# One kernel for a decoder layer: row statistics and the joint of mixer and feed-forward rearranged

## The reference

```python
x = x + mamba_block(layernorm(x), ...)                # "front" stage of the kernel
x = x + mlstm(layernorm(x), ctx, ctx, ...)            # "mixer"
x = x + ffn(layernorm(x), w_gate, w_up, w_down)       # "feed-forward"

# mlstm, per batch and head (4 heads of 64 channels, 256 tokens)
C = (q k^T / 8) * exp(log_D - max_log_D)
h = (C / max(|sum C|, exp(-max_log_D))) v
h_norm = (h - mean(h)) / sqrt(mean((h - mean(h))**2) + 1e-5)  # over the 64 channels
out = h_norm * (1 + out_w)

# ffn: every linear quantises both operands to a 4-bit grid in blocks of 16
layernorm(x) = (x - mean) / sqrt(var + 1e-5)          # per token, over 256 channels
gate, up = fp4_linear(x, w_gate), fp4_linear(x, w_up) # 704 hidden columns
y = fp4_linear(silu(gate) * up, w_down)
```

## Time and profile before

| | us |
|---|---|
| median of 3 runs | 604.32 (603.13 to 605.93) |
| profiled execution | 606.77, of which the span of instructions 605.1 |
| PE busy | 567.9 (94%) |
| DVE busy | 446.4 (74%) |
| ACT busy | 270.1 (45%) |
| POOL busy | 144.6 (24%) |

### The profile page before, as it was taken

How to read it: one execution, slowest core, us unless ns; L and a number is a source line. 1 busy time by engine, 2 the same in 40 slices (tenths; PEclk the granted TensorE clock), 3 DMA queues, 4 the chain that set the end, 5 groups by cost and what they waited for, 6 DMA issues and landing times. The chain is left out here.

```text
span 605.1 us, 9377 instructions
## 1 busy us (share of the span) xinstructions
PE 567.9 (94%) x2995; PEld 459.4 (76%) x2995; DVE 446.4 (74%) x990; ACT 270.1 (45%) x565; POOL 144.6 (24%) x209
## 2 busy tenths in 40 slices
PE   7989998999999899999999999989959899999995
PEld 6766666788888788888888888877855577777774
DVE  6986598379888324755655857575788999999994
ACT  2655877785788422222111112434434444444431
POOL 4120001134545021210110010005775222122200
PEclk8989999799999999999999999998977999999999
DMA  8300101000000093000000000011100000000000
GB/s 301 121 1 18 35 15 39 22 25 5 6 7 0 2 298 90 1 1 0 1 1 1 1 0 1 4 43 33 35 2 0 2 17 17 14 12 17 18 19 26
DMA packets 21392, 18.90 MB, mean 31 GB/s; under 512 B 12008, under 2 KB 20584, under 8 KB 20968
## 3 DMA queue, kind: packets, MB, share of 16 engines
q1 hardware_dynamic: 20920, 18.36, 9.5%
q10 hardware_dynamic: 432, 0.03, 0.1%
HBM read 16.04 MB, written 2.34 MB: 30 GB/s over the span
## 5 line engine op out<-in xcount | busy, mean ns | idle before, releaser
L923 PE MATMUL ps<-xnT,w_fc 128*128 128x256 f32 x512 | 112.8, 380 | 0.0
L923 PEld LDWEIGHTS ps<-xnT,w_fc 128*128 128x128 f32 x512 | 96.5, 190 | 12.7
L1658 PE MATMUL ps<-w_fc,scores 128*128 128x352 f32 x256 | 82.3, 476 | 1.5 <-ACT scores L1747 1.5
L1658 PEld LDWEIGHTS ps<-w_fc,scores 128*128 128x128 f32 x256 | 48.9, 196 | 29.0 <-ACT scores L1747 3.6
L1166 ACT ACTIVATE xs<-ps 128x512 f32<-128x512 f32 x32 | 19.1, 597 | 95.8 <-PE ps L923 75.7
L1279 DVE SCALAR_TENSOR_TENSOR fold<-xpad,conv_w,fold 128x256 f32<-128x256 f32 x120 | 50.9, 481 | 2.4 <-ACT fold L1068 1.6
L1677 PE MATMUL ps<-u_res,hT 128*128 128x256 f32 x192 | 44.2, 380 | 3.8 <-DVE scores L1856 2.8
L1677 PEld LDWEIGHTS ps<-u_res,hT 128*128 128x128 f32 x192 | 36.3, 190 | 11.3 <-issue 3.0
L806 PE MATMUL ps<-xnT,fold 128*128 128x256 f32 x160 | 39.2, 393 | 1.6 <-ACT xpad L1062 0.8
L806 PEld LDWEIGHTS ps<-xnT,fold 128*128 128x128 f32 x160 | 30.7, 198 | 9.5 <-issue 3.6
L813 PE MATMUL ps<-fold,xnT 128*128 128x512 f32 x64 | 36.8, 708 | 0.0
(11 more groups left out here) (299 smaller groups left out, 1208.8 us busy)
## 6 DMA issues: line engine op xcount, KB each, us to landing
zs<-in_ffn_w SPq DMA_DIRECT2D x1, 2112.0 KB, 10.9
x_res<-in_x SPq DMA_DIRECT2D x8, 256.0 KB, 7.6
w_fc<-in_w_fc SPq DMA_DIRECT2D x1, 2048.0 KB, 10.3
xnT<-in_ctxT SPq DMA_DIRECT2D x8, 256.0 KB, 3.1
xs<-in_ctx SPq DMA_DIRECT2D x16, 128.0 KB, 3.0
xs<-in_ctxT SPq DMA_DIRECT2D x8, 256.0 KB, 3.1
out<-scores SPq DMA_DIRECT2D x16, 128.0 KB, 1.7
fold<-in_w_in SPq DMA_DIRECT2D x2, 580.0 KB, 6.6
```

The lines of the kernel that those rows point to most:

```text
L923: last = pe.matmul(bank[half + r][:, i * S:(i + 1) * S], m.w_fc1[:, kk, col:col + P], m.xnT[:, b, kk * S:(kk + 1) * S], start=(kk == 0), s ...
L1658: last = pe.matmul(bank[1 + j][:, 0:HALF], xT[:, p, k * P:(k + 1) * P], m.w_gu[:, k, j * HALF:(j + 1) * HALF], start=(k == 0), stop=(k == ...
```

## The change

Three things are done.

- The row statistics of the feed-forward's layer norm move from its rounds into the mixer, a batch (two tiles) at a time: on DVE `row_stats` (lag 4, two statistics and two aggregates) between `weights` and `normalise`; on POOL `row_rstds` (lag 4, one addition, one power and two multiplications) ahead of `rstds`. The results are kept for all 16 tiles. The rounds have no statistics left, and POOL has nothing in them.
- `squares` becomes eight Squares of 64 columns, each with an accumulated sum. DVE's `variance` is gone.
- `pipelines` is gone. The joint is written out engine by engine. On DVE the first two tiles' `step_x` parts are spread over mixer steps 6 to 8; rounds 3 and 4 are cut and stand around mixer steps 9 and 10; round 5 stands ahead of the last `row_stats` (step 11); rounds 6 to 15 are the loop. On PE `gate_up(0)` stands ahead of the last batch's `sums`.

```diff
--- before.py
+++ after.py
...
-def pipelines(eng, units, stages, next_units, next_stages, begin, overlap):
...
@@ -1516,7 +1499,7 @@
-    BEGIN, OVERLAP = B - 1, 5
+    ROUNDS_APART = 6
...
-    st = sb("f_st", [P, 2, 6])
-    mv = sb("f_mv", [P, 2, 2])
-    ve = sb("f_ve", [P, 2, 1])
-    rstd = sb("f_rstd", [P, 2, 1])
-    shift = sb("f_shift", [P, 2, 1])
+    st = sb("f_st", [P, 2, C, 6])
+    mv = sb("f_mv", [P, T, 2])
+    ve = sb("f_ve", [P, T])
+    rstd = sb("f_rstd", [P, T])
+    shift = sb("f_shift", [P, T])
...
+    def rounds(eng, stages, first):
+
+        for r in range(first, ROUNDS_APART):
+            step(T, stages, r)
+        steady(eng, T, stages, ROUNDS_APART, T)
+        for r in range(T, T + depth_of(stages)):
+            step(T, stages, r)
...
@@ -1698,10 +1689,23 @@
-        forward = [(turn_x, 2), (lambda t, p: turn_down(0 if t == 0 else 2) if round_at(t) and t < 2 else None, 2),
-                   (turn_h, 4), (gate_up, 2), (lambda t, p: turn_down(1) if round_at(t) and t == 0 else None, 2),
-                   (down, 4)]
-        pipelines(pe, B, mixer, T, forward, BEGIN, OVERLAP)
+        forward = [(turn_x, 2), (turn_h, 4), (gate_up, 2), (down, 4)]
+        for k in range(B):
+            step(B, mixer, k)
+        last, p = B - 1, (B - 1) % 2
+        scores1_even(last, p)
+        scores0(last, p)
+        scores1_odd(last, p)
+        turn_x(0, 0)
+        sums(last - 1, 1 - p)
+        turn_down(0)
+        gate_up(0, 0)
+        sums(last, p)
+        turn_x(1, 1)
+        turn_down(1)
+        gate_up(1, 1)
+        turn_down(2)
+        rounds(pe, forward, 4)
...
         def squares(b, p):
             act.wait_ge(s["h_read"], LEAD + b + 1)
+            act.wait_ge(s["v_rstd"], LEAD + b - 1)
             act.wait_ge(s["v_ready"], LEAD + b)
-            act.activation(sq[:].rearrange("p g e -> p (g e)"), h[:, p, :, :].rearrange("p g e -> p (g e)"),
-                           ACT.Square).then_inc(s["sq_ready"], 1)
-
+            for i in range(C * XH):
+                last = act.activation(sq[:, i, :], h[:, p, i, :], ACT.Square, accum_out=var[:, p, i:i + 1])
+            last.then_inc(s["v_ready"], 1)
...
-            act.activation(xf[:, p, :], row(m.x_res, t), ACT.Identity, bias=shift[:, p, :], scale=rstd[:, p, :])\
+            act.activation(xf[:, p, :], row(m.x_res, t), ACT.Identity, bias=shift[:, bass.ds(t, 1)],
+                           scale=rstd[:, bass.ds(t, 1)])\
                .then_inc(f["xf_norm"], 1)
...
-        forward = [(turned_x, 2), (lambda t, p: save_down(0 if t == 0 else 2) if round_at(t) and t < 2 else None, 2),
-                   (turned_h, 4), (lift_x, 1), (lift_h, 3), (silu, 2),
-                   (lambda t, p: save_down(1) if round_at(t) and t == 0 else None, 2), (norm, 0)]
-        pipelines(act, B, mixer, T, forward, BEGIN, OVERLAP)
+        forward = [(turned_x, 2), (turned_h, 4), (lift_x, 1), (lift_h, 3), (silu, 2), (norm, 0)]
+        for k in range(B - 1):
+            step(B, mixer, k)
+            if k == B - 3:
+                norm(0, 0)
+            if k == B - 2:
+                norm(1, 1)
+                lift_x(0, 0)
+        last, p = B - 1, (B - 1) % 2
+        exps(last, p)
+        turned_x(0, 0)
+        squares(last - 2, p)
+        save_down(0)
+        squares(last - 1, 1 - p)
+        lift_x(1, 1)
+        norm(2, 0)
+        silu(0, 0)
+        turned_x(1, 1)
+        save_down(1)
+        squares(last, p)
+        lift_x(2, 0)
+        lift_h(0, 0)
+        silu(1, 1)
+        save_down(2)
+        norm(3, 1)
+        rounds(act, forward, 4)
...
-        def variance(b, p):
-            dve.wait_ge(s["sq_ready"], LEAD + b + 1)
-            dve.wait_ge(s["v_rstd"], LEAD + b - 1)
-            dve.tensor_reduce(var[:, p, :], sq[:], AX.X, ALU.add).then_inc(s["v_ready"], 1)
-
...
-        def tile_stats(t, p):
-            dve.wait_ge(s["x2_ready"], LEAD + t + C - p)
-            carry(dve, m)
-            dve.bn_stats(st[:, p, :], row(m.x_res, t)).then_inc(f["f_stats"], 1)
-
-        def tile_mean(t, p):
-            dve.wait_ge(f["f_stats"], LEAD + t + 1)
-            carry(dve, m)
-            dve.bn_aggr(mv[:, p, :], st[:, p, :]).then_inc(f["f_mv_ready"], 1)
+        def row_stats(b, p):
+            dve.wait_ge(s["x2_ready"], LEAD + C * (b + 1))
+            for c in range(C):
+                last = dve.bn_stats(st[:, p, c, :], m.x_res[:, C * b + c, :])
+            last.then_inc(f["f_stats"], 1)
+            dve.wait_ge(f["f_stats"], LEAD + b + 1)
+            for c in range(C):
+                last = dve.bn_aggr(mv[:, C * b + c, :], st[:, p, c, :])
+            last.then_inc(f["f_mv_ready"], 1)
...
-        first = [stage for k in range(5) for stage in ((step_x(k), 1), (step_h(k), 3))]
-        last = [stage for k in range(6, 9) for stage in ((step_x(k), 1), (step_h(k), 3))]
+        def parts(begin, end):
+            return [stage for k in range(begin, end) for stage in ((step_x(k), 1), (step_h(k), 3))]
+
+        def rows_steps(t, begin, end):
+            for k in range(begin, end):
+                step_x(k)(t, t % 2)
...
-        mixer = [only(3, lambda: chain.a_tokens(dve, TOKENS[0]).then_inc(m.gates_done, 1)),
+        begin = [only(3, lambda: chain.a_tokens(dve, TOKENS[0]).then_inc(m.gates_done, 1)),
                  only(4, lambda: chain.nm_tokens(dve, TOKENS[1]).then_inc(m.gates_done, 1)),
-                 (lambda b, p: weights(b, p, 0), 1), (lambda b, p: weights(b, p, 1), 1), (variance, 3),
-                 only(1, lambda: chain.sums(dve, *SECOND_HALF)), (normalise, 2),
-                 (scale, 3), only(2, lambda: chain.maxima(dve))]
-        forward = [(product, 3), *first, (tile_stats, 0), (output, 5), (tile_mean, 0), *last]
-        pipelines(dve, B, mixer, T, forward, BEGIN, OVERLAP)
+                 (lambda b, p: weights(b, p, 0), 1), (lambda b, p: weights(b, p, 1), 1), (row_stats, 4),
+                 only(1, lambda: chain.sums(dve, *SECOND_HALF))]
+        end = [(normalise, 2), (scale, 3), only(2, lambda: chain.maxima(dve))]
+        forward = [(product, 3), *parts(0, 5), (output, 5), *parts(6, 9)]
+        for k in range(B + 1):
+            step(B, begin, k)
+            if k == B - 2:
+                rows_steps(0, 0, 3)
+            elif k == B - 1:
+                rows_steps(0, 6, 9)
+            elif k == B:
+                rows_steps(1, 0, 3)
+            step(B, end, k)
+            if k == B - 2:
+                rows_steps(0, 3, 5)
+            elif k == B:
+                rows_steps(1, 3, 9)
+        step(T, [(product, 3), *parts(0, 1)], 3)
+        step(B, begin, B + 1)
+        step(B, end, B + 1)
+        step(T, [*parts(1, 9)], 3)
+        step(T, [(product, 3), *parts(0, 2)], 4)
+        step(B, begin, B + 2)
+        step(B, end, B + 2)
+        step(T, [*parts(2, 9)], 4)
+        step(T, forward, 5)
+        step(B, begin, B + 3)
+        rounds(dve, forward, 6)
...
-        def tile_rstd(t, p):
-            pool.wait_ge(f["f_mv_ready"], LEAD + t + 1)
-            carry(pool, m)
-            pool.tensor_scalar(ve[:, p, :], mv[:, p, 1:2], LN_EPS, None, ALU.add).then_inc(f["f_ve_ready"], 1)
-            pool.wait_ge(f["f_ve_ready"], LEAD + t + 1)
-            pool.tensor_tensor(rstd[:, p, :], ve[:, p, :], m.minus_half[:, 0:1], ALU.pow).then_inc(f["f_rstd_ready"], 1)
-            pool.wait_ge(f["f_rstd_ready"], LEAD + t + 1)
-            pool.wait_ge(f["xf_norm"], LEAD + t - 1)
-            carry(pool, m)
-            pool.tensor_scalar(shift[:, p, :], mv[:, p, 0:1], rstd[:, p, :], -1.0, ALU.mult, ALU.mult)\
-                .then_inc(f["f_shift_ready"], 1)
-
-        mixer = [(rstds, 3), (residual, 3)]
-        forward = [(tile_rstd, 0)]
-        pipelines(pool, B, mixer, T, forward, BEGIN, OVERLAP)
+        def row_rstds(b, p):
+            here = slice(C * b, C * (b + 1))
+            pool.wait_ge(f["f_mv_ready"], LEAD + b + 1)
+            pool.tensor_scalar(ve[:, here], mv[:, here, 1], LN_EPS, None, ALU.add).then_inc(f["f_ve_ready"], 1)
+            pool.wait_ge(f["f_ve_ready"], LEAD + b + 1)
+            pool.tensor_tensor(rstd[:, here], ve[:, here], m.minus_half[:, 0:C], ALU.pow).then_inc(f["f_rstd_ready"], 1)
+            pool.wait_ge(f["f_rstd_ready"], LEAD + b + 1)
+            for t in range(C * b, C * (b + 1)):
+                pool.tensor_scalar(shift[:, t:t + 1], mv[:, t, 0:1], rstd[:, t:t + 1], -1.0, ALU.mult, ALU.mult)\
+                    .then_inc(f["f_shift_ready"], 1)
+
+        mixer = [(row_rstds, 4), (rstds, 3), (residual, 3)]
+        for k in range(B + 4):
+            step(B, mixer, k)
```

## The result

The changed kernel takes 621.03 us (median of 4, 616.59 to 622.75), the kernel before 605.01: a ratio of 1.026, 95% interval 1.0213 to 1.0306, 16.0 us slower. Forecast was 618.8. Medians in this document are over all executions of a kernel, while the ratios leave out the few that were in a slower state. The profiled execution took 619.5 us with a span of 617.8, where before it was 606.8 and 605.1 [the table ahead]. The two profiles differ by 12.7 only, because the untouched front stage differs from run to run: the first `scale` starts at 411.95 before and at 410.26 after. I call it the stretch.

The account below looks back on a forecast made before the run. PE bounds the mixer, waits the joint, DVE the rounds. POOL's loop, Squares and joint add 14.9 us, rounds take off 0.3: +14.6, from the median 604.3 to 618.8 us; range 609 to 627.

Parts of the forecast that it names:

- The loop through POOL: Mixer: row_stats, row_rstds, rstds, scale and residual wait in a ring, 8.6 us a turn against PE's 5.96.
- The rival of GpSimd's length alone: Mixer: only POOL's own length binds, a step costs 7.3 us, total 612; chance 0.12.
- Until scale(4): Mixer steps 4 to 7: scale(4) at 451.3 where it was at 438.24, +13.1 us.
- the Squares in step 4: ACT in mixer step 4: exp_nm, and nm_tokens with it, slips by 2.9 us (bounds 1.0 and 5.8).
- The `step_x` parts of step 7: DVE in the mixer: parts put into steps 6 and 7 lie beside POOL's work and cost nothing.
- The Squares: ACT: 0.42 us each with the read, eight 3.4 us a batch (bounds 1.5 to 6.3), mostly hidden.
- The rival of a cheap accumulation: ACT: accumulation costs no time of its own, eight Squares take 1.2 us, total 615.4; chance 0.10.
- The joint: Mixer's end into the first rounds: loses 1.8 us more than the mixer's 13.1, round 6 starting at 504.2.
- quantisation beside `residual(6)` and `residual(7)`: DVE in rounds 3 and 4: slowed beside POOL's residual, 1.3 us and 1.0 us added.
- it let `product(0)` wait for `squares(6)` ahead of `lift_x(1)`: Step 8: squares(6) ends at 461.6, then lift_x(1), norm(2), table load and silu(0) until 464.7.
- The dearer joint: ACT's Squares at 0.79 us each, or PE at half clock through gate_up(0) and gate_up(1): 624 to 628; chance 0.11.
- The rounds: Feed-forward: removing statistics saves 0.03 us a round, 0.3 us in ten, because DVE then waits for lift_h.

Follow-up runs that it names:

- Turned order: Changed kernel with POOL's mixer order rstds, row_rstds, residual: 606.5 us, ratio 1.003; or rstds, residual, row_rstds: 608.5 us, ratio 1.004.
- doubled power: Changed kernel with row_rstds computing its power twice, the first into a spare tile: 625.5 us, ratio 1.032.
- left-out statistics: Changed kernel without row_stats and row_rstds, rows normed with constants, ScalarE's norm waiting for the batch's residual: 600.1 us, ratio 0.994.
- rows last: Changed kernel with POOL's mixer order rstds, residual, row_rstds: 608.5 us, ratio 1.004.
- one Square: Changed kernel with one Square of 128x512 a batch on ScalarE and the reduction on VectorE again: 619.3 us, ratio 1.026.
- the kernel before with the Squares: Kernel before with only the eight accumulating Squares a batch added and VectorE's reduction removed: 609.2 us, ratio 1.006.

## Why the prediction was right

- **The loop through POOL** (8.6 us a turn forecast): right in mechanism and nearly in size: 8.3 for two turns, 9.0 for the third. `row_rstds` is 1.72 instead of 1.9, most of it because the gap ahead of its multiplications is 0.10 instead of 0.24, and the handover from VectorE to GpSimd is 0.09 instead of 0.2. Turned order, doubled power and left-out statistics each moved the time in the direction that the loop has. The loop is passed seven times from `scale(0)` to `scale(7)`, as the doubled power shows; the bounds of the range were worked out with six. The rival of GpSimd's length alone is excluded by rows last.
- **Until scale(4)**: 39.4 us from `scale(0)` forecast (26.3 + 13.1), 37.4 measured. The term mis-sized is the Squares in step 4: 2.9 forecast, 1.4 measured (`nm_tokens` 5.04 us behind `scale(0)` instead of 3.65, and the first turn 1.4 shorter with one Square). The `step_x` parts of step 7 were put at nothing, but that turn is 0.75 longer than the two before it: one of them, the conversion to integers, takes 1.25 us beside GpSimd's multiplication instead of 0.29 and holds up `row_stats` by 0.4, and GpSimd's operations beside the others are 0.3 longer.
- **The Squares**: I took 0.42 us for each, 0.24 was measured. The rival of a cheap accumulation had the better size (0.15). The figure worked out from the Trainium skill's page "ScalarE: Activation LUTs", section "What ACT_TABLE_LOAD costs", an estimate of 0.146 from start to start, lies 0.09 below the measurement where mine lies 0.18 above. The read starts 0.14 us behind its Square and the next Square 0.10 behind the read, so they overlap; what a Square of 64 columns takes without the read, no run shows.
- **The joint**: 52.9 us forecast from `scale(4)` to round 6, 54.6 measured. The term mis-sized is quantisation beside `residual(6)` and `residual(7)`: 2.3 forecast. VectorE after, the row's and the hidden row's part 3 in round 3:

```profile
469.33 1.05 DVE L326 SCALAR_TENSOR_TENSOR xq_v<-xq_inv,scores 128x256 f32<-128x256 f32 x1
470.30 1.95 DVE L326 SCALAR_TENSOR_TENSOR hq_v<-hq_inv,hf 128x704 f32<-128x704 f32 x1
```

They take 1.05 and 1.95 us instead of 0.36 and 0.88 alone; this comes twice (in round 4 again 1.27 and 1.96), 3.8 us in all. The prediction had one wait of the joint wrong: it let `product(0)` wait for `squares(6)` ahead of `lift_x(1)`. The Squares ended at 456.45, and ScalarE then waited 1.80 us for VectorE's conversion, again slow beside GpSimd (whose multiplication lies at 456.67 to 458.06):

```profile
456.97 1.24 DVE L328 TENSOR_SCALAR xq_g<-xq_v 128x256 int32<-128x256 int32 x1
...
458.24 0.51 ACT L1760 ACTIVATE xq_g<-xq_g,grid_bias 128x256 f32<-128x256 f32 x1 [1.80 <-DVE xq_g L328]
```

From `scale(5)` to `product(0)` it was 5.4 us against a forecast 4.8, by another path. The dearer joint's own causes, dearer Squares or `gate_up` at half clock, did not come about at `product(0)`: `silu(0)` followed its table load at once.
- **The rounds**: 0.03 us each forecast, 0.02 to 0.03 measured, with the wait of 0.29 in its place.
- The errors cancelled: -2.0 up to `scale(4)`, +1.7 in the joint. The stretch was forecast at 92.3 and measured at 92.0, and that this came so close is luck. Half clock in steps 4 and 5 was in no rival; in the kernel before with the Squares those two steps were 3.2 us longer. In the changed kernel PE was at half clock too (about 418 to 421, and 438 to 445), but it hid under the loop: in all seven turns `scale` still waited 1.2 to 3.8 us for `rv`, and VectorE waited for PE only for `nm_tokens` (4.4), and 1.1 us otherwise.

## What to carry to other kernels

Before work moves into a stage with room on its engine, follow the waits of that engine's order for one turn: here GpSimd had idle time of 1.33 us a step, and 1.7 us of work ahead of the wrong operation, with 1.0 us on VectorE in the same loop, cost 2.3 us a step. Behind it the step cost 1.1 more than before, and of that 0.9 came even in a step without the GpSimd work, through VectorE's own order (`row_stats` and the `step_x` parts behind it): when one loop is opened, sum up the next one. Work that stands in a wait is free, and taking it out brings the wait back. A small operation that another engine waits for should not be queued behind a new series.

## What the runs showed of the hardware

Eight accumulating Squares of 64 columns start 0.24 us apart, although each shows 0.24 to 0.30 us and its read 0.18 to 0.25. VectorE's 128x704 multiplication beside a 128x512 addition on GpSimd took 1.95 us instead of 0.88, and its 128x256 conversion beside a 128x512 multiplication there 1.25 instead of 0.29. The same untouched front stage ended up to 8 us apart between profiled runs (`scale(0)` at 404.1 to 412.4), with a mean granted clock from 390 us to `scale(0)` between 0.74 and 1.00, which is as much as most edits here are worth: a stretch inside the change tells more than the span.
